# Moving a quarter of the z projection of a delta head from behind the V transposes into the last step of the solve before it

## What is computed

```python
z = jnp.einsum('bth,vh->btv', x, W_z)
# conv + silu of the projected q, k, v; q and k are normalised
def step(state, inp):
    q_t, k_t, v_t, b_t, d_t = inp
    state = state * d_t[..., None, None]
    Sk = jnp.einsum('bhi,bhij->bhj', k_t, state)
    delta = (v_t - Sk) * b_t[..., None]
    state = state + jnp.einsum('bhi,bhj->bhij', k_t, delta)
    o = jnp.einsum('bhi,bhij->bhj', q_t, state)
    return (state, o)
state, o = jax.lax.scan(step, state0, (tm(q), tm(kk), tm(v), tm(beta), tm(decay)))
y = o * jax.nn.silu(zz)
y = y * jax.lax.rsqrt(jnp.mean(y * y, axis=-1, keepdims=True) + 1e-06) * norm_w
out = jnp.einsum('btv,ov->bto', y.reshape(B, T, VDIM), W_out)
```

## Time and profile before

| | |
|---|---|
| median of 3 runs | 1877.07 us (1877.06 to 1877.42) |
| the profiled execution, its own time | 1876.01 us |
| its span | 1874.1 us |
| mean granted clock of TensorE | 0.98 |
| PE busy | 1717.0 us (92%) |
| weight loads (PEld) | 1328.4 us (71%) |
| DVE busy | 1443.1 us (77%) |
| ACT busy | 1123.9 us (60%) |
| POOL busy | 732.4 us (39%) |

### The profile page before, as it was taken

How to read it: one execution, slowest core, us unless ns; L and a number is a source line. 1 busy time by engine, 2 the same in 40 slices (tenths; PEclk the granted TensorE clock), 3 DMA queues, 4 the chain that set the end, 5 groups by cost and what they waited for, 6 DMA issues and landing times.

```text
span 1874.1 us, 34411 instructions
## 1 busy us (share of the span) xinstructions
PE 1717.0 (92%) x13208; PEld 1328.4 (71%) x13208; DVE 1443.1 (77%) x2389; ACT 1123.9 (60%) x2154; POOL 732.4 (39%) x474
## 2 busy tenths in 40 slices
PE   7899999999989978989989999899899998999976
PEld 5676767676756757768678687686776876867765
DVE  8788888888856477877878788778787887787853
ACT  3344443434344465876867778768677787676762
POOL 2222222222231253643725626437256264372540
PEclk9999999999999978999999999999999999999988
DMA  3010101010013101011010110110101101101000
GB/s 138 34 65 32 64 32 64 32 64 32 33 53 90 49 1 35 24 35 57 25 35 24 36 57 24 35 53 28 35 24 35 57 24 35 55 27 35 7 2 23
DMA packets 51449, 75.44 MB, mean 40 GB/s; under 512 B 3392, under 2 KB 41792, under 8 KB 51184
## 3 DMA queue, kind: packets, MB, share of 16 engines
q1 hardware_dynamic: 51312, 73.55, 12.1%
HBM read 72.29 MB, written 1.25 MB: 39 GB/s over the span
## 4 chain that ended last, share of the span: by engine, by line
PE 41%; DVE 13%; ACT 10%; issue 5%; POOL 2%; ACTq 0%; POOLq 0%; DVEq 0%
PE bank L909 6%; PE bank L731 6%; DVE d_sil L1333 5%; PE bank L864 3%; DVE d_X L1387 3%; PE bank L751 3%; PE bank L761 2%; PE bank L852 2%; PE bank L802 2%; PE bank L812 2%; POOL d_dec L1652 2%; PE bank L885 2%; ACT d_V L1121 2%; DVE d_Rb L1403 2%; PE bank L816 2%
## 5 line engine op out<-in xcount | busy, mean ns | idle before, releaser
L1652 POOL TENSOR_TENSOR d_dec<-d_dec,d_qk 128x384 f32<-128x384 f32 x128 | 161.9, 1290 | 511.9 <-DVE d_N L1368 511.9
L1333 DVE SCALAR_TENSOR_TENSOR d_sil<-d_pre,d_w,d_sil 128x1024 f32<-128x1024 f32 x192 | 300.1, 1563 | 5.9 <-ACT d_pre L1093 5.7
L189 PE MATMUL bank<-xnT,a_w 128*128 128x512 f32 x512 | 237.2, 597 | 0.0
L731 PE MATMUL bank<-xnT,d_w 128*128 128x512 f32 x480 | 235.6, 619 | 0.1
L1387 DVE CAST_PREDICATED d_X<-tables_sb,bank 128x512 bf16<-128x512 int32 x192 | 134.4, 700 | 129.6 <-PE bank L802 122.4
L489 POOL TENSOR_TENSOR a_hidc<-a_hid,a_comb 128x512 f32<-128x512 f32 x32 | 44.4, 1387 | 294.9 <-DVE a_hid L336 294.9
L1159 ACT ACTIVATE d_T<-bank 128x512 bf16<-128x512 f32 x160 | 96.7, 605 | 101.9 <-PE bank L812 100.1
L189 PEld LDWEIGHTS bank<-xnT,a_w 128*128 128x128 f32 x512 | 90.9, 192 | 78.6 <-issue 78.6
L1644 POOL TENSOR_TENSOR x_sb<-x_sb,d_yrs 128x1024 f32<-128x1024 f32 x32 | 73.7, 2325 | 160.5 <-DVE d_yrs L1446 160.5
L731 PEld LDWEIGHTS bank<-xnT,d_w 128*128 128x128 f32 x480 | 85.2, 195 | 67.0 <-issue 67.0
L864 PE MATMUL bank<-d_W,d_N 128*128 128x128 f32 x1024 | 130.8, 281 | 2.1 <-DVE d_W L1408 1.9
(11 more groups left out here) (210 smaller groups left out, 4424.9 us busy)
## 6 DMA issues: line engine op xcount, KB each, us to landing
d_dec<-decay_scratch SPq DMA_DIRECT2D x32, 512.0 KB, 5.9
a_w<-w SPq DMA_DIRECT2D x16, 897.0 KB, 4.6
d_w<-w SPq DMA_DIRECT2D x16, 776.0 KB, 4.6
a_comb<-comb_scratch SPq DMA_DIRECT2D x16, 512.0 KB, 5.6
d_dec<-decay_scratch SPq DMA_DIRECT2D x32, 256.0 KB, 6.2
d_wo<-w SPq DMA_DIRECT2D x16, 256.0 KB, 2.9
f_w<-w SPq DMA_DIRECT2D x8, 256.0 KB, 4.1
tables_sb<-tables SPq DMA_DIRECT2D x1, 1056.0 KB, 10.2
```

Source lines behind the costliest of these rows:

```text
L189: last = pe.matmul(psum[bank][:, :], wq(slot, part, k), xnT[:, k, half * HALF:(half + 1) * HALF], start=(k == 0), stop=(k == KT - 1))
L731: last = pe.matmul(psum[bank][:, :], cols(slot, (c * KT + k) * P, P), xnT[:, k, h * HALF:(h + 1) * HALF], start=(k == 0), stop=(k == KT - 1))
L1333: dve.scalar_tensor_tensor(sil[c][:, :, :], pre[c % 2][:, :, tap:tap + S], cols(slot, OC + 4 * c + tap, 1), sil[c][:, :, :], ALU.mult, ALU ...
L1652: pool.tensor_tensor(g, g, qk[b % 2][:, :, :], ALU.mult).then_inc(s["p_done"], 1)
```

## The change

For heads 1 to 15 the two halves of quarter 2 of z are issued one head earlier, in the sixth step of the previous head's solve: the first half between the two applies, the second behind them, ahead of `outputs`. Head 0 keeps its call behind `turn_v`. The wait for `kss_done` and the increment of `z_ready` move with the work, and no other engine's program changes.

```diff
--- before.py
+++ after.py
@@ -913,7 +913,8 @@
             def body(j, slot, i):
                 nxt = after(j, slot, i)
                 turn_v(i)
-                project_z(slot, i, 2)
+                if isinstance(i, int) and i == 0:
+                    project_z(slot, i, 2)
                 pe.wait_ge(s["sil_done"], i * 4 + 2)
                 products(i, 0)
                 products(i, 1)
@@ -947,6 +948,7 @@
                     between[2], behind[2], closing[2] = [q(0, 1)], [q(1, 0)], [q(1, 1)]
                     between[3] = [z(1, 0)]
                     between[4] = [z(1, 1)]
+                    between[5], behind[5] = [z(2, 0)], [z(2, 1)]
                 invert(i, fill)
                 for c in range(2):
                     for a in range(3):
```

## The result

| | before | changed |
|---|---|---|
| median | 1877.07 us (4 runs, 1875.79 to 1877.42) | 1885.41 us (4 runs, 1885.01 to 1887.94) |
| profiled execution, its time / its span | 1876.01 / 1874.1 us | 1885.64 / 1883.6 us |
| ratio | | 1.0049, 95% interval 1.0036 to 1.0061 |

The change makes the kernel slower, by 8.3 us between the medians; the ratio says 9.2 us, with 6.8 to 11.5 as its interval. The direction was forecast, the size was not: 6.3 us were forecast, with a range whose upper end, 1885.8, the ratio (1.0049 x 1877.07 = 1886.3) passes by half a microsecond; the median itself, 1885.41, lies just inside.

A forecast was written before the change was run, and what follows sets the result against it. DVE, with ACT and POOL, was taken to bound the kernel from first matrices to first level; 1.09 - 0.58 - 0.09 = 0.42 us per border, 15 borders, 6.3 us, gives 1883.4 us; range 1881.6 to 1884.8, widened to 1879.0 to 1885.8.

The forecast's parts named there:

- What bounds: Between the first matrices and the first level DVE, with ACT and POOL work hanging on it, sets the pace; PE waits.
- X: The start of DVE's first matrices in a head, forecast to come 0.42 us later.
- the tanh chain: ACT's tanh and copies from the V transposes to DVE's second gate: keeps its length, starts 1.09 us later.
- The delay of the outputs: Sixth solve step: the moved halves make the outputs, and the V transposes with them, 1.09 us later.
- From T to X: From the V transposes (T) to DVE's first matrices: 4.3 us instead of 5.0, as DVE's 0.58 us wait for PE goes.
- PE's waits: PE's wait for ACT's copies before the last products: from 0.54 to 1.4 us, 8.1 to some 21 over the run.
- The regular head: Each border between heads costs 0.42 us more, so a head takes 75.4 us instead of 75.0.
- what lies behind: PE's queue behind the last products, up to the next solve's sixth step: unchanged, only 0.42 us later, costed at nothing.
- PE's queue deciding: Rival: PE's 0.44 us lead per border at the second products' end reaches the first level; 6.6 us faster, 1870.5; chance 0.08.
- No change: Rival: some of the 0.42 us is lost before level one; 1880.2 us with half lost, 1877.1 with all; chance 0.12.
- the full delay: Rival: ACT's first copies set the pace through POOL, 1.09 us passes per border; 16.4 us, 1893.4 us; chance 0.03.

The follow-up runs named there:

- the run that has it alone: Kernel before, with quarter 2 computed a second time in the sixth step and the call behind the V transposes kept: 1896.62 us, ratio 1.0108.
- the reordered one without idle matmuls: The reordered kernel with the two idle matmuls ahead of the first level removed: 1875.91 us, ratio 0.9993 against the kernel before.
- the half: Kernel before with only the first half of quarter 2 moved into the sixth step, the second kept behind the V transposes: 1877.31 us, ratio 0.9998.
- the reordered kernel: Half moved plus idle matmuls; second half behind first two products, gate of quarter 1 behind first matrices, tanh of quarter 2 behind ACT's first copies: 1865.49 us.

## Why the prediction was right and wrong

- **What bounds.** That DVE, with ACT and POOL behind it, sets the pace from X to the first level was right; the exchange of two DVE operations changed the head by 0.27 us, and leaving out the whole quarter did not bring X nearer than the tanh chain lets it.
- **The delay of the outputs.** Forecast 1.09, measured 1.11 in the changed kernel, and heads longer by 1.11 in the run that has it alone.
- **From T to X.** Forecast 4.31, measured 4.32. The pitch of 0.60 between a gate and the next operation is 1190.69 to 1191.29 in the changed kernel too. With a pipe that has to empty first (the Trainium skill, VectorE: DVE Perf Modes, section "The DRAIN you can't avoid") it would be the row's 0.69, and the rows disagree with that; the prediction left out that the same section has a next operation that is not held start earlier, which is what the rows show.
- **PE's waits.** Forecast 1.4 ahead of the last products, measured 1.31; 21 us over the run, measured 19.6.
- **The regular head.** Forecast 0.42, measured 0.45: the term was right. Two slips in the working change nothing: the gate's excess over the pitch stands there once as 0.08 and once as 0.09, and DVE's share of a head, 59.33 in the row, as 59.4.
- **The step that failed** is the sentence on what lies behind: "I cost that at nothing: all of it starts 0.42 later and ends 0.42 later." It took the clock of TensorE for given because the window of one head showed 1.00. Four more heads than before fell to the low level in the profiled pair, 2.71 us, and the missing 0.38 us of the last head (its gain of 0.66 up to the last products, 0.28 at the end) went the same way: a block of its L909 records took 3.13 us of the queue at a granted clock of 0.57, where before it took 2.76 at 0.65. With both, the forecast for the profiled execution, 1876.01 + 6.3, would have been 1885.4 us, against 1885.64 measured. The part that was forecast was right by its mechanism; what was missing is the clock. The sign that was there to be read is head 13 of the kernel before, 75.60 us among heads of 75.0; I had written that the heads repeat closely enough for one to stand for all.
- **The rivals.** PE's queue deciding: PE's lead did arrive (its wait grew) and was worth nothing. No change, and the full delay: neither happened. The forecast's own range, 1881.6 to 1884.8, had bounds for every term but this one, and the 1.0 us added above it for costs taken as unmoved was less than the 3.1 us that the clock took. That filling PE's gaps "should pay" was read too widely out of the page that the prediction names for this rival: its section goes on to have what the gap waits for start sooner, and this change starts it later.

The rule that comes nearest is in the Trainium skill, TensorE: Matmul & The Clock Gate, section "Part 1: The HAM clock gate": the array's clock is released by activity and gated when there is too little of it. The rows agree with that: the clock fell behind waits and stayed up where idle matmuls stood in one of them. Its advice against long single gaps would not have warned here: the longest wait ahead of a fall in the changed kernel was 1.31 us, and 1.04 us in head 7 of the reordered one without idle matmuls. The same part also tells of a kernel in which frequent short idle stretches between groups of matmuls made the clock swing between its two levels, and that is what these rows resemble.

## What to carry to other kernels

On a queue that is mostly busy, ask of each move two things: which chain on the other engines starts at the instruction that it delays, and how much of the delay those chains hand on. Here moving work ahead of the event that starts ACT's and DVE's chain cost 1.11 us and gave back only the 0.66 us for which DVE had waited; half the move costs 0.25 for the same 0.66. And take the length of every repeat, not of one: a few repeats that are longer by a constant amount, with a low granted clock, say that the clock is part of the cost, and that what a move gains may be taken back by it until something fills one of the waits.

## What the runs showed of the hardware

- TensorE's clock fell to 1.2 GHz for a few microseconds in the first levels of a head behind waits of 1.31, 1.04 and 0.93 us in the changed kernel, and behind waits of 1.04 and 0.93 us alone in the reordered one without idle matmuls; the same waits stood in heads where it did not fall. Such a fall cost a head 0.6 to 0.8 us, less than the 1.55 us lost in the slow records of head 3, since other waits shortened.
- 0.86 us of matmuls without use in one of these waits kept the clock up in all 14 heads of each of the four kernels that had them, and were worth 7.5 us beside the half (1877.31 to 1869.86) and 10.4 us in the reordered kernel (1875.91 to 1865.49). In the last head, at the low clock and with a wait of 0.52 us to fill, they took 1.81 us and cost about 1.1.
- How many heads fall is not told by the length of the waits alone: 1 of 14 before, 6 of 14 with the same waits and longer heads, 5 and 4 in two profiles of the changed kernel, 10 with half the work moved, 13 with the work left out or reordered. Falls in neighbouring heads stood 75.1 us apart in every kernel that had such neighbours, so heads whose length with a fall is near that fell again and again. The length was not changed by itself.
